# One result sum instead of two, and the expert loop's inputs fetched one unit earlier

## The chip, the cores and the metric

The kernel runs on one core of one Trainium2 chip. The time is the device time of a run in microseconds, the median of three runs. The profile is of one execution; its span goes from the first to the last instruction that was recorded.

## The reference

A batch of 16 sequences of 112 tokens of width 512 (1792 tokens) goes through two layers. The first is a cross-attention to 375 context rows, added to x. The second is a mixture of 64 experts:

```python
logits = x @ gate_weight.T                 # x is the layernormed token, 64 experts
top_val, top_idx = top_k(softmax(logits), 8)
rerouted = mapping[top_idx]                # the weaker 4 may be moved to a similar expert
gu = ragged_dot(xs, gate_up_proj)          # xs: the tokens of each expert, 512 -> 2*192
hact = silu(gate) * up
y = ragged_dot(hact, down_proj)            # 192 -> 512
out = zeros.at[tok].add(y * w)             # each token gets a sum over its experts
x = x + out
```

The last step is what the change is about: one token's row is added to by up to eight experts.

## The kernel before

**First part (0 to about 197 us).** The 16 sequences go through attention, gating and placing. SP stores x + attention to `out_rows` and the normed tokens to `normed_tokens`, and POOL enters each (token, weight) into the list of its expert in DRAM with 112 indirect DMAs (`enter`, L592).

**Second part, the expert loop.** Experts are ranked by how many tokens they have, and slot r of the program takes the expert of rank r. A *unit* is one expert: 17 units of three tiles (2 of 128 rows each, 8 of 112, 7 of 96) and then 46 of two tiles (17 of 128, 16 of 112, 12 of 96, 1 of 80). At the end a loop adds a tile of 128 rows for what did not fit (here one turn). All products are done in three passes on a high and a low part of each operand, so each unit needs its weights and tokens split: ACT copies the high part (`w1_high` L1052, `w2_high`, `x_high`, `h_high` L1030), DVE subtracts to get the low one (`w1_low` L909, `w2_low`, `x_low`, `h_low`).

For each unit:

- SP loads its list (`load_list`), its first weights `raw1` (768 KB, three DMAs, L484) and its second weights `raw2` (384 KB, L490 and L491).
- POOL gathers the tokens' rows into `xg` (L608). PE turns them (`turn_rows`), multiplies by the first weights in three groups m = 0, 1, 2 (`gate_up`, L1223 to L1225) and by the second (`down`).
- ACT takes `silu` of group 0 and of group 2, DVE multiplies (`h_gate` after group 1, `h_rest` L886 and L887 after group 2).
- ACT scales the result by the token's weight into `ys` (`y_out`, L1040), and POOL scatters `ys` with an indirect DMA that adds to DRAM (L617). `ys` has two buffers, so `y_out` of a unit waits until the scatter of the unit two before has landed.

The order on each engine is the order of the program: round r issues a stage of unit r, of r + 1 and so on, and an instruction that waits holds all behind it on its engine. Two adds to the same row may not be under way together. Before the change, units take turns between two sums: even ones add to `out_rows` (semaphore `scattered[0]`), odd ones to a second DRAM array `second_sum` (`scattered[1]`), which SP cleared in the first part. So the scatter of unit u waits for that of u - 2:

```python
def sums(self):
    return self.slot % 2
split_wait(pool, scattered[u.sums()], u.landed_before())
```

When all have landed, POOL adds `second_sum` to `out_rows` with one DMA of 3.5 MB (L644, `merged`), and the scatter of the last loop's tile (L638) waits for that. The code line above has a second effect: `load_list` of unit r + 4 reuses the list buffer of unit r - 4, waits until that unit's scatter has landed (L472), and stands on SP ahead of the weights of unit r + 2.

## Time and profile before

| | |
|---|---|
| median of three runs | 839.45 us (837.8 to 840.26) |
| profiled execution, first to last instruction | 805.3 us |
| PE, PEld, DVE, ACT, POOL busy | 676.6, 560.5, 541.6, 450.7, 516.2 us |
| mean granted TensorE clock | 0.936 |
| expert loop, first scatter to last scatter | 236.59 to 768.89 us |

The page gives the profiled execution's time as its span; the runs' own times hold some 34 us more (839.45 - 805.3), which lie before the first or after the last instruction. Busy shares are means over a first part that is bound by other things than the expert loop; the loop has to be read by stage.

### The profile page before, as it was taken

What the parts mean: (1) busy time and instruction counts of PE and PEld (TensorE: products, weight loads), DVE (VectorE), ACT (ScalarE), POOL (GpSimd) and SP (SyncE); (2) the same over time, 40 slices, a digit from 0 to 9 for tenths busy, and PEclk for the clock granted to TensorE, in tenths of its full rate; (3) what the DMA queues carried; (4) which work ended last, traced back from release to release, by engine and by line L of the source; (5) the groups of instructions that cost most, each with busy time, mean ns of one, the idle gap of its engine ahead of it and who ended that gap; (6) DMA issues with size and microseconds to landing.
All of it is one profiled execution on the core that took longest, in us unless ns stands there. A gap on an engine that the chain in (4) does not pass through costs nothing. (4 is left out here: it accounts for less than half of the span.)

```text
span 805.3 us, 15215 instructions
## 1 busy us (share of the span) xinstructions
PE 676.6 (84%) x4278; PEld 560.5 (70%) x4278; DVE 541.6 (67%) x1213; ACT 450.7 (56%) x891; POOL 516.2 (64%) x461
## 2 busy tenths in 40 slices
PE   4999999630599999999998998999988998989730
PEld 2555565320589999888988888878877977878630
DVE  5699898861276667776677777776767777767611
ACT  3444454310366666666775766757666676666610
POOL 6037777776738877887766666676657666666421
PEclk9999999855599999999999999999999999999965
DMA  8999999505659999999999999999999999999576
GB/s 304 349 313 332 322 330 301 170 12 159 177 154 220 244 240 237 239 247 255 247 268 256 268 241 259 245 245 258 236 260 217 250 236 245 233 246 232 107 132 152
DMA packets 107557, 189.93 MB, mean 236 GB/s; under 512 B 33521, under 2 KB 35441, under 8 KB 106065
## 3 DMA queue, kind: packets, MB, share of 16 engines
q1 hardware_dynamic: 74274, 125.61, 50.2%
q0 software_dynamic: 33200, 63.35, 38.9%
q8 instruction: 35, 0.57, 0.3%
q14 instruction: 48, 0.39, 0.2%
HBM read 143.40 MB, written 56.24 MB: 248 GB/s over the span
## 5 line engine op out<-in xcount | busy, mean ns | idle before, releaser
L1223 PE MATMUL bank<-xh,w1h 128*128 128x256 f32 (+7 forms) x768 | 229.3, 299 | 21.4 <-DVE h L887 21.2
L1224 PE MATMUL bank<-xl,w1h 128*128 128x256 f32 (+7 forms) x768 | 220.5, 287 | 0.0
L1225 PE MATMUL bank<-xh,w1l 128*128 128x256 f32 (+7 forms) x768 | 220.4, 287 | 0.0
L608 POOL DMA_INDIRECT xg<-normed_tokens,list x145 | 159.3, 1099 | 62.5 <-issue 55.9
L1223 PEld LDWEIGHTS bank<-xh,w1h 128*128 128x128 f32 x768 | 147.5, 192 | 27.0 <-issue 26.7
L617 POOL DMA_INDIRECT out_rows<-ys,list x73 | 116.7, 1599 | 72.9 <-ACT ys L1040 60.4
L903 DVE TENSOR_TENSOR xl<-bank,xh 128x448 fp32r<-128x448 f32 (+3 forms) x145 | 84.3, 616 | 115.1 <-ACT xh L1047 115.0
L592 POOL DMA_INDIRECT list_table<-token,slot x112 | 112.4, 1004 | 69.7 <-ACT token L1001 35.9
L617 POOL DMA_INDIRECT second_sum<-ys,list x70 | 111.2, 1589 | 64.5 <-ACT ys L1040 43.5
L1224 PEld LDWEIGHTS bank<-xl,w1h 128*128 128x128 f32 x768 | 147.9, 193 | 0.1
L1225 PEld LDWEIGHTS bank<-xh,w1l 128*128 128x128 f32 x768 | 147.6, 192 | 0.0
L909 DVE TENSOR_TENSOR w1l<-raw,w1h 128x1536 fp32r<-128x1536 f32 x65 | 114.5, 1762 | 39.9 <-ACT w1h L1052 39.9
L1205 PE MATMUL bank<-ident,xg 112*128 112x112 f32 (+3 forms) x580 | 76.7, 268 | 58.9 <-DMA xg<-normed_tokens,list 56.8
L1030 ACT CAST hh<-h 128x512 fp32r<-128x512 f32 (+6 forms) x64 | 39.0, 610 | 150.4 <-DVE h L887 150.4
L1205 PEld LDWEIGHTS bank<-ident,xg 112*128 112x128 f32 (+3 forms) x580 | 63.8, 144 | 76.3 <-DMA xg<-normed_tokens,list 42.0
L1052 ACT CAST w1h<-raw 128x1536 fp32r<-128x1536 f32 x65 | 97.4, 1499 | 6.4 <-DMA raw<-in_w 6.4
L1047 ACT CAST xh<-bank 128x448 fp32r<-128x448 f32 (+3 forms) x145 | 70.8, 537 | 47.6 <-PE bank L1205 47.6
L1040 ACT ACTIVATE ys<-bank,list 112x512 f32<-112x512 f32 (+3 forms) x143 | 89.3, 680 | 2.2 <-PE bank L1241 2.2
L894 DVE TENSOR_TENSOR hl<-h,hh 128x512 fp32r<-128x512 f32 (+6 forms) x64 | 43.5, 680 | 46.9 <-DVE h L887 44.9
L1236 PE MATMUL bank<-w2h,hh 128*112 128x512 f32 (+3 forms) x144 | 57.0, 396 | 5.5 <-DVE hl L894 5.5
L1241 PE MATMUL bank<-w2h,hl 128*112 128x512 f32 (+3 forms) x144 | 57.0, 396 | 0.0
L1238 PE MATMUL bank<-w2h,hl 128*112 128x512 f32 (+3 forms) x144 | 56.9, 395 | 0.0
(204 smaller groups left out, 1084.7 us busy)
## 6 DMA issues: line engine op xcount, KB each, us to landing
raw<-in_w SPq DMA_DIRECT2D x195, 256.0 KB, 4.7
raw<-in_w2a SPq DMA_DIRECT2D x65, 256.0 KB, 5.0
ctxT_s<-in_ctxT SPq DMA_DIRECT2D x16, 768.0 KB, 7.3
ctx_s<-in_ctx SPq DMA_DIRECT2D x16, 768.0 KB, 8.8
raw<-in_w2b SPq DMA_DIRECT2D x65, 128.0 KB, 5.9
list_table<-blank SPq DMA_DIRECT2D x30, 256.0 KB, 7.6
x_in<-in_x SPq DMA_DIRECT2D x16, 224.0 KB, 4.5
out_rows<-x SPq DMA_DIRECT2D x16, 224.0 KB, 8.8
```

What stands on the lines that cost most here:

```text
L592: pool.indirect_dma_start(table, bass.IndirectOffsetOnAxis(ap=slot8[b.four][:, k:k + 1], axis=0), token[b.four][:, k, :], None).then_inc(t ...
L608: pool.indirect_dma_start(xg[u.on(XGS)][0:u.m, t, :], None, normed, bass.IndirectOffsetOnAxis(ap=lists[u.on(LISTS)][0:u.m, t, 0:1], axis=0 ...
L617: pool.indirect_dma_start((out, second)[u.sums()], bass.IndirectOffsetOnAxis(ap=lists[u.on(LISTS)][0:u.m, t, 0:1], axis=0), ys[u.on(2)][0: ...
L903: v.tensor_tensor(xl[u.on(2)][:, :, part], turned(u, t), xh[u.on(2)][:, :, part].bitcast(F32), ALU.subtract).then_inc(xl_s, 1)
L909: v.tensor_tensor(w1l[u.on(2)][:].rearrange("p c f -> p (c f)"), raw1[u.on(RAW1)][:], w1h[u.on(2)][:].rearrange("p c f -> p (c f)").bitcas ...
L1040: a.activation(ys[u.on(2)][0:u.m, t, :], y_bank(u, t)[0:u.m, :], ACT.Copy, scale=of_row).then_inc(ys_s, 1)
L1047: a.copy(xh[u.on(2)][:, :, t * u.m:(t + 1) * u.m], turned(u, t)).then_inc(xh_s, 1)
L1052: a.copy(w1h[u.on(2)][:].rearrange("p c f -> p (c f)"), raw1[u.on(RAW1)][:]).then_inc(w1h_s, 1)
L1205: mm = pe.transpose(turned(u, t)[:, c, :], xg[u.on(XGS)][0:u.m, t, c * P:(c + 1) * P], ident[0:u.m, 0:u.m])
L1223: pe.matmul(bank[m][:, 0:W], wh, mh, start=(c == 0), stop=False)
L1224: pe.matmul(bank[m][:, 0:W], wh, ml, start=False, stop=False)
L1225: mm = pe.matmul(bank[m][:, 0:W], wl, mh, start=False, stop=(c == DK - 1))
```

## The change

- `second_sum`, its clearing, the merge and the second semaphore are gone. Every scatter adds to `out_rows`, and the scatter of a unit waits until **all** tiles of the units before it have landed. The last loop's scatter has a semaphore of its own (`over_added`).
- Buffers: `raw1` 3 to 4, `raw2` 2 to 3, lists 8 to 12, `xg` 3 to 4. SP loads lists 6 rounds ahead (4 before), `raw1` 4 (2), `raw2` 2 (1). POOL gathers 3 ahead (2).
- ACT and DVE split the first weights of unit r + 2 (r + 1 before), and do so late in the round. DVE does `h_rest` ahead of `w2_low`.
- PE's group m of a unit waits only for what frees its own bank; before, group 1 waited for all of `h` of the unit before.

The last three pieces below are DVE's order, ACT's order and PE's `gate_up`.

```diff
-SUM_TILES = [sum(nt for nt, m in RANKED[i::2]) for i in range(2)]
-RAW1, LISTS, XGS = 3, 8, 3
+RAW1, RAW2, LISTS, XGS = 4, 3, 12, 4
...
     def landed_before(self):
-        tiles = sum(nt for v, (nt, m) in enumerate(RANKED[:self.slot]) if v % 2 == self.slot % 2)
-        return tiles * 16 if not self.loop else (self.n - self.slot + tiles) * 16
+        return self.t0 * 16
...
-            for n in range(4):
+            for n in range(6):
                 load_list(Unit(n))
             for r in range(STATIC):
-                early_stage(load_list, r + 4)
-                if r > 0:
-                    early_stage(load_w1, r + 2)
-                early_stage(load_w2, r + 1) if r > 0 else None
+                early_stage(load_list, r + 6)
+                early_stage(load_w1, r + 4)
+                early_stage(load_w2, r + 2)
...
             def scatter(u):
-                split_wait(pool, scattered[u.sums()], u.landed_before())
+                wait(pool, scattered, u.landed_before())
                 for t in range(u.nt):
-                    pool.indirect_dma_start((out, second)[u.sums()], bass.IndirectOffsetOnAxis(ap=lists[u.on(LISTS)][0:u.m, t, 0:1], axis=0),
+                    pool.indirect_dma_start(out, bass.IndirectOffsetOnAxis(ap=lists[u.on(LISTS)][0:u.m, t, 0:1], axis=0),
...
             for r in range(STATIC + 2):
-                early_stage(gather, r + 2)
+                early_stage(gather, r + 3)
                 stage(scatter, r - 2)
...
-            for i in range(2):
-                pool.wait_ge(scattered[i], SUM_TILES[i] * 16)
-            pool.dma_start(out[0:TOK, :], second[0:TOK, :], accum_op=ALU.add, max_dma_last_dim=8192).then_inc(merged, 16)
...
             for r in range(STATIC):
                 early_stage(x_low, r + 1, (0, 1))
-                early_stage(w1_low, r + 1)
                 stage(h_gate, r)
                 early_stage(x_low, r + 1, (2,))
+                stage(h_rest, r)
                 stage(w2_low, r)
-                stage(h_rest, r)
+                early_stage(w1_low, r + 2)
                 stage(h_low, r)
...
             for r in range(STATIC):
                 early_stage(x_high, r + 1, (0, 1))
-                early_stage(w1_high, r + 1)
                 stage(silu_gate, r)
                 early_stage(x_high, r + 1, (2,))
                 stage(w2_high, r)
                 stage(silu_rest, r)
+                early_stage(w1_high, r + 2)
                 stage(h_high, r)
                 stage(y_out, r - 1)
...
-                if m == 0:
-                    wait(pe, silu_s, u.n * 2)
-                else:
-                    wait(pe, h_s, u.n * 3)
+                if u.loop or u.n > 0:
+                    if m == 0:
+                        pe.wait_ge(silu_s, u.n * 2 - 1)
+                    elif m == 1:
+                        pe.wait_ge(h_s, u.n * 3 - 2)
+                    else:
+                        pe.wait_ge(h_s, u.n * 3)
```

On POOL, in the middle of the expert loop (units of two tiles of 112 rows), three units in a row before; `ys`, `list` and `xg` carry their buffer's number, and the brackets hold the semaphores waited for:

```order
L617 DMA second_sum<-ys1,list5 1792x512 [waits ys_s,scattered1]
L617 DMA second_sum<-ys1,list5 1792x512 [waits ys_s]
L608 DMA xg0<-normed_tokens,list2 112x512 [waits xT_ps,list_in2]
L608 DMA xg0<-normed_tokens,list2 112x512
L617 DMA out_rows<-ys0,list6 1792x512 [waits ys_s,scattered0]
L617 DMA out_rows<-ys0,list6 1792x512 [waits ys_s]
L608 DMA xg1<-normed_tokens,list3 112x512 [waits xT_ps,list_in3]
L608 DMA xg1<-normed_tokens,list3 112x512
L617 DMA second_sum<-ys1,list7 1792x512 [waits ys_s,scattered1]
```

and the same place now:

```order
L598 DMA out_rows<-ys0,list0 1792x512 [waits ys_s,scattered]
L598 DMA out_rows<-ys0,list0 1792x512 [waits ys_s]
L589 DMA xg2<-normed_tokens,list6 112x512 [waits xT_ps,list_in6]
L589 DMA xg2<-normed_tokens,list6 112x512
L598 DMA out_rows<-ys1,list1 1792x512 [waits ys_s,scattered]
L598 DMA out_rows<-ys1,list1 1792x512 [waits ys_s]
L589 DMA xg3<-normed_tokens,list7 112x512 [waits xT_ps,list_in7]
L589 DMA xg3<-normed_tokens,list7 112x512
```

Scatters and gathers alternate as before, with the gather for one unit further ahead; what changed is that every scatter's first tile waits for the one `scattered`.

On ACT, at the same place before, one unit from `x_high` to `y_out`:

```order
L1047 CAST xh0<-bank4 128x4x96 [waits xT_ps,gu_ps]
L1047 CAST xh0<-bank3 128x4x96 [waits xT_ps]
L1052 CAST w1h0<-raw1_2 128x1536 [waits gu_ps,w1_in2]
L1019 ACTIVATE sg<-bank0 128x224 [waits h_s,gu_ps]
L1058 CAST w2h1<-raw2_1 128x512 [waits y_ps,w2_in1,gu_ps]
L1059 CAST w2h1<-raw2_1 64x512
L1024 ACTIVATE sg<-bank2 64x224 [waits gu_ps]
L1030 CAST hh1<-h 128x2x224 [waits y_ps,h_s]
L1040 ACTIVATE ys0<-bank7,list0 112x512 [waits y_ps,scattered0]
L1040 ACTIVATE ys0<-bank5,list0 112x512 [waits y_ps]
```

and now:

```order
L1031 CAST xh0<-bank4 128x4x96 [waits xT_ps,gu_ps]
L1031 CAST xh0<-bank3 128x4x96 [waits xT_ps]
L1001 ACTIVATE sg<-bank0 128x224 [waits h_s,gu_ps]
L1043 CAST w2h1<-raw2_1 128x512 [waits y_ps,w2_in1,gu_ps]
L1044 CAST w2h1<-raw2_1 64x512
L1006 ACTIVATE sg<-bank2 64x224 [waits gu_ps]
L1036 CAST w1h1<-raw1_3 128x1536 [waits gu_ps,w1_in3]
L1012 CAST hh1<-h 128x2x224 [waits y_ps,h_s]
L1024 ACTIVATE ys0<-bank7,list0 112x512 [waits y_ps,scattered]
L1024 ACTIVATE ys0<-bank5,list0 112x512 [waits y_ps]
```

The cast of the first weights (`w1h`) moved from ahead of the first `silu` to behind the second.

## Rows read from the trace of the kernel before

**Rows 1.** windows, by kind of unit (first scatter to first scatter)

```profile
core 0: us, PE busy (x) PEld busy (x) DVE busy (x) ACT busy (x) POOL busy (x), PEclk, DMA share, GB/s
236.59:401.83 165.24, 165.03 (x1076) 148.35 (x1075) 115.00 (x167) 114.55 (x202) 132.09 (x98) 1.00 1.01 239
401.83:545.62 143.79, 132.37 (x929) 119.18 (x928) 104.78 (x153) 96.27 (x172) 93.79 (x69) 1.00 1.01 255
545.62:676.74 131.12, 119.39 (x866) 106.10 (x866) 93.79 (x144) 87.24 (x162) 85.86 (x65) 0.99 0.98 242
676.74:767.18 90.44, 79.93 (x572) 68.64 (x571) 61.04 (x98) 58.48 (x111) 55.17 (x41) 0.98 0.87 206
```

**Rows 2.** timeline, one two-tile unit: start us, us, engine and line, what, idle before

```profile
501.67 0.62 ACT L1030 CAST hh<-h 128x512 fp32r<-128x512 f32 x1 [2.80 <-DVE h L887]
501.78 0.36 PE L1223 MATMUL bank<-xh,w1h 128*128 128x256 f32 x1 [0.80 <-DVE h L887]
502.20 1.26 ACT L1040 ACTIVATE ys<-bank,list 128x512 f32<-128x512 f32 x2
503.74 1.62 POOL L617 DMA_INDIRECT second_sum<-ys,list  x1 [2.09 <-ACT ys L1040]
504.29 1.51 ACT L1052 CAST w1h<-raw 128x1536 fp32r<-128x1536 f32 x1
505.83 1.76 DVE L909 TENSOR_TENSOR w1l<-raw,w1h 128x1536 fp32r<-128x1536 f32 x1 [0.51 <-ACT w1h L1052]
509.71 0.42 DVE L887 TENSOR_TENSOR h<-sg,bank 64x256 f32<-64x256 f32 x1
```

**Rows 3.** waits in the two-tile stages: who, for whom, us in total, times, longest

```profile
PE bank L1223 <- DVE h L887: 21.2, 30, 0.9
```

**Rows 4.** waits of the DMA queue on SP, same columns, 250 to 765 us

```profile
SPq L472 <- DMA second_sum<-ys,list: 46.2, 22, 3.0
SPq L472 <- DMA out_rows<-ys,list: 45.1, 24, 3.1
```

**Rows 5.** timeline, POOL and SP: a scatter's last tile, the next list load

```profile
497.19 1.59 POOL L617 DMA_INDIRECT out_rows<-ys,list  x1 [0.30 <-issue]
505.10 0.35 SPq L477 DMA_DIRECT2D list<-list_table  x1
...
646.25 1.49 POOL L617 DMA_INDIRECT out_rows<-ys,list  x1 [0.30 <-issue]
654.91 0.35 SPq L477 DMA_DIRECT2D list<-list_table  x1
...
637.99 1.49 POOL L617 DMA_INDIRECT second_sum<-ys,list  x1 [0.30 <-issue]
642.75 0.50 SPq L491 DMA_DIRECT2D raw<-in_w2b  x1
644.04 0.35 SPq L477 DMA_DIRECT2D list<-list_table  x1
```

**Rows 6.** timeline, POOL, the last scatter and the merge

```profile
768.89 1.41 POOL L617 DMA_INDIRECT out_rows<-ys,list  x1 [0.30 <-issue]
773.31 1.09 POOL L644 DMA_DIRECT2D out_rows<-second_sum  x1 [3.00 <-DMA out_rows<-ys,list]
```

**Rows 7.** chain that ended last, 766 to 806 us: start us, us, what

```profile
776.17 10.21 DMA list<-list_table
787.47 8.81 DMA xg<-normed_tokens,list
799.47 1.76 DVE w1l L909
```

**Rows 8.** one line's DMAs, list loads (first) and gathers: issue to landing

```profile
DMA to landing us min/median/max: 1.8/3.8/10.2
DMA to landing us min/median/max: 3.3/6.3/8.8
```

**Rows 9.** page, section 5: POOL's table entries in the first part

```profile
L592 POOL DMA_INDIRECT list_table<-token,slot x112 | 112.4, 1004 | 69.7 <-ACT token L1001 35.9
```

More of the change, by code:

```diff
@@ L121, in turn_of_tile @@
         return earlier if not self.loop else self.n - self.slot + earlier
-    def sums(self):
-        return self.slot % 2
     def landed(self, back):
-        upto = max(self.slot - back + 1, 0)
-        tiles = sum(nt for v, (nt, m) in enumerate(RANKED[:upto]) if v % 2 == (self.slot - back) % 2)
-        return tiles * 16
+        return TILES_BEFORE[max(self.slot - back + 1, 0)] * 16
     def landed_before(self):
-        tiles = sum(nt for v, (nt, m) in enumerate(RANKED[:self.slot]) if v % 2 == self.slot % 2)
-        return tiles * 16 if not self.loop else (self.n - self.slot + tiles) * 16
+        return self.t0 * 16
     def units_freed(self, ring):
@@ L196, in program @@
         row = sb("row", [P, 1])
-        zeros = sb("zeros", [P, D])
         blank = sb("blank", [P, BLANKS, LINE], I32)
@@ L223, in program @@
         raw1 = [sb(f"raw1_{i}", [P, DK * 2 * F]) for i in range(RAW1)]
-        raw2 = two("raw2_", [P, 2, D])
+        raw2 = [sb(f"raw2_{i}", [P, 2, D]) for i in range(RAW2)]
         w1h = [sb("w1h0", [P, DK, 2 * F], F32R)]
@@ L469, in load_list @@
                 else:
-                    wait(sp, scattered[u.sums()], u.landed(LISTS))
+                    wait(sp, scattered, u.landed(LISTS))
                 if u.slot < STATIC:
@@ L532, in _ @@
                                     pattern=[[-1, P]], channel_multiplier=1).then_inc(const_pool, 1)
-            nc.gpsimd.memset(zeros[:], 0.0).then_inc(const_pool, 1)
             nc.gpsimd.memset(blank[:], 0).then_inc(cleared, 1)
@@ L623, in _ @@
             gather(Unit(1))
+            gather(Unit(2))
             for r in range(STATIC + 2):
[L625 removed]
+                early_stage(gather, r + 3)
                 stage(scatter, r - 2)
             def keep_list(u):
[L629 removed]
+                split_wait(pool, list_in[u.on(LISTS)], (u.turn(LISTS) + 1) * 16)
                 nc.gpsimd.tensor_copy(over_list[:], lists[u.on(LISTS)][:, 0, 0:1]).then_inc(kept, 1)
@@ L1035, in y_out @@
                     split_wait(act, kept, (u.n - STATIC + 1) * KEPT)
-                wait(act, scattered[u.sums()], u.landed_before() if u.loop else u.landed(2))
+                    act.wait_ge(scattered, TILES_BEFORE[STATIC - 1] * 16)
+                else:
+                    wait(act, scattered, u.landed(2))
                 for t in range(u.nt):
```

66 lines of the change are left out of this document (32 added, 34 removed).

## The prediction, made before the result was known

> **What bounds the kernel now.** I read the waits and the windows by stage first, then the timeline of one unit, then SP's own waits, and the end of the chain last.
>
> While units have three tiles, PE is the bound: busy 165.03 of 165.24 us [rows 1]. In the three two-tile stages it is busy 132.37 of 143.79, 119.39 of 131.12 and 79.93 of 90.44 us, so 33.7 us are idle there, 21.2 of them before group 1 of `gate_up`, waiting for the `h` of the unit before [rows 3]. The timeline shows why [rows 2]. At 501.67 ACT starts `h_high`, then `y_out` and `x_high`, and the weight cast at 504.29 ends at 505.80; DVE's `w1_low` starts at 505.83, and the last `h` starts 3.9 us later at 509.71 and ends at 510.13, when the next `h_high` may start. That is a loop of ACT and DVE of 8.5 us, with nothing in it that PE or POOL could shorten. PE joins it with 0.80 us of idle.
>
> POOL waits too, 2.09 us for `ys`, but its scatters are not free [rows 2]. SP's list load waited 91.3 us in 46 places until a scatter had landed [rows 4]: landings come late. How late is read from the list load behind each wait. Without a wait, the list's DMA starts 0.79 us after the DMA ahead of it has been issued (642.75 + 0.50 = 643.25, then 644.04). So the scatter whose last tile was issued from 497.19 to 498.78 landed at 505.10 - 0.79 = 504.31, 5.5 us after its issue ended; the one of 647.74 landed at 654.12, 6.4 us after. Before 644.04 SP had not waited, so the tile issued until 639.48 (637.99 + 1.49) had landed by 643.25, at most 3.8 us after [rows 5]. The last scatter, with nothing else on the queues, landed no more than 3.0 us after 770.30 [rows 6]. The DMA engines' share is 1.01, 1.01, 0.98 and 0.87 [rows 1].
>
> **The change, part by part.** The sum is made on the span of 805.3 us and carried to the median of 839.45, since the 34 us outside the span hold none of the changed code.
>
> *One sum: the scatter chain.* Before, unit u waited for u - 2, which had two unit times to land. Now it waits for u - 1. From one scatter's start to the next there are then: (a) POOL's start after the wait ends. Not shown for this wait; the nearest is `ys`: first tile done at 502.20 + 0.68 = 502.88 (half of the 1.26 us and the overlap), scatter at 503.74, so 0.86 us [rows 2]. (b) The issue: 1.62 + 0.30 + 1.59 = 3.5 us for two tiles, 1.6 x 3 + 0.6 = 5.4 us for three [rows 2, 5]. (c) The landing L after the issue. The gathers, 2 or 3 of about 1.1 us, are issued inside L and cost nothing as long as L is over 3 to 4 us.
>
> L is the unknown. Its ends are 3.0 (empty queues) and 6.4 us. The samples under load lie at 5.5 and 6.4 with one at or under 3.8 [rows 5, 6]. I take 4.5, and 3.9 for the 96-row units, where the share is 0.87. That is below the middle of the loaded samples for two reasons. In a chain, no scatter packet is under way for some 3 us of each turn, which lets the weights through; and units come less often, which thins the load. Weights no longer stand behind the landing on SP (the list load waits for six units back), so they are issued when `w2_low` is done, about 7 us after the last `y_out`, and the 768 KB then run partly beside the next scatter. This is why I don't go lower.
>
> - 17 three-tile units: 0.86 + 5.4 + 4.5 = 10.76, times 17 = 182.9 us; before 165.2: +17.7.
> - 17 units of 2 x 128: 8.87, 150.8; before 143.8: +7.0.
> - 16 of 2 x 112 (issue 3.33): 8.69, 139.0; before 131.1: +7.9.
> - 12 of 2 x 96 (issue 3.2, L 3.9): 7.96, 95.5; before 90.4: +5.1.
>
> Together +37.7 us. Each 0.1 us of L is worth 62 x 0.1 = 6.2 us.
>
> The Trainium skill (DMA: Bandwidth & Descriptors, "Anatomy of one DMA — SWDGE (gpsimd) path") gives about 2.0 us plus bytes / 436e3 for a DMA from GpSimd, most of the 2 us being the receipt of the write; for a tile of 262 KB that is 2.6 us. The last scatter agrees with it (3.0 at most), the loaded ones don't (5.5, 6.4) [rows 5, 6]. With L = 2.6 the chain would be under PE's time everywhere, which is the first rival. The same page ("Latency and other measured facts") lets the access time of DRAM grow from 0.2 to 2 us at high load; that is in the sense of the loaded samples.
>
> *The reordering on ACT, DVE and PE.* It takes the weight cast and `w1_low` out of the loop of 8.5 us. What is left per unit of 2 x 128 is ACT's and DVE's own work: 96.27 / 17 = 5.7 and 104.78 / 17 = 6.2 us against PE's 132.37 / 17 = 7.8 [rows 1]. So PE would be the bound and 33.7 us would go. But the chain, 8.87 us, is longer than 7.8, so nothing of it is seen: `y_out` waits for the landing two units back, and ACT, then DVE, then PE stand behind it. With three tiles PE needs 165.03 / 17 = 9.7 us against the chain's 10.76. I cost this part at zero; it is worth up to -33.7 us if the chain is not the bound.
>
> *Fetching ahead.* Lists, weights and gathers are not what any long wait in the loop is for, so 0. At the start, PE does unit 0's group 0 before it turns unit 1's rows (up to -2 us), and 1.9 MB of weights instead of 0.8 run beside the first gathers (up to +2 us). I take 0. The SP stores of zeros and POOL's memset went from a part in which POOL's 112 table entries follow each other 1.3 us apart to the end (141 us; idle between them 33.8 without the first wait) [rows 9]: 0.
>
> *The end.* From 770.30, the end of the last scatter's issue, to 805.30 are 35.0 us: 3.0 of landing, the merge, then the over loop's bookkeeping for a next turn that is prefetched: list load 10.21, gather 8.81, then PE, ACT and DVE up to 801.23 [rows 6, 7]. Without the merge: POOL's copies and SP's list load come at once (776.17 - 773.31 = 2.9 after 770.30), the list takes 2.5 (between the least, 1.8, and the median, 3.8 [rows 8]), 1.1 to the gather (787.47 - 786.38), the gather 4 (least 3.3), 4.95 until `w1_low` ends, 4.07 to the end: 19.4, so -15.6 us. The last scatter lies beside this.
>
> Sum: 37.7 - 15.6 = +22: span 827, time 861 us.
>
> **Rivals.**
>
> 1. *The landing shortens to its unloaded value and PE becomes the bound.* The chain's turn for two tiles is under PE's 7.8 us if L is under 7.8 - 0.86 - 3.5 = 3.4. For it: the 3.0 us of the last scatter, the one of at most 3.8, and weights that are no longer bunched behind a landing. Against: a DMA share of 1.01 in all of the loop's first two stages [rows 1]; going from 8.5 to 7.8 us a unit asks for 9% more of it. Time: 839.45 - 33.7 - 15.6 - 1 = 789 us.
> 2. *The chain binds, but with L of 3.4 to 4.1.* The end's gain is larger than what the chain costs: 806 to 837 us.
> 3. *The chain binds with the landing as it is in the loaded samples, 5.1 or more*: 861 + 62 x 0.6 = 898 us. For it: two of three samples. Against: the load must fall when units come less often.
> 4. *No change:* the chain costs just what the end gives, L = 4.15 (0.35 less than 4.5).
>
> The forecast itself is the case on the slower side of the point where it turns: mean L above 4.15 us.
>
> **How the numbers follow.** Forecast, L from 4.2 to 5.0 (842 to 892 us): 0.50. Rival 1: 0.20. Rival 2: 0.14. Rival 3: 0.10. Rival 4: 0.06. The runs before spread over 2.5 us, so a change of 0.3% is about the least that can be told. Faster 0.34, same 0.06, slower 0.60. The range of 8 in 10 goes from 796, in the upper half of rival 1, to 893; the forecast's own range is 842 to 892.
>
> **What would show it.** If I am right, POOL's scatter waits mostly for a scatter's landing and no longer for `ys`; the turn from scatter to scatter is 10 to 11 us with three tiles and 8.4 to 9.2 with two, constant over widths where PE's would shrink; PE is idle already in the three-tile stages, and ACT's `ys` waits for a landing. The wait before group 1 for `h` is gone from the list in either case. If POOL waits for `ys` and PE stays 98% busy in the two-tile stages, rival 1 holds. The end from the last scatter is 19 us instead of 35 in all cases; over 25 would make that step wrong. The whole is wrong if the mean landing, read from scatter end to scatter start less 0.86, is under 4.1.

## The result, and the profile after

| | before | after |
|---|---|---|
| time, median (lowest to highest) | 838.62 us (837.38 to 840.26, 4 runs) | 868.30 us (865.72 to 871.27, 4 runs) |
| ratio after to before | | 1.0354, 95% interval 1.0326 to 1.0383 |

The change makes the kernel 3.5% slower: 868.3 us, where 861 was forecast.

The page of the kernel after: its span, then from section 4 the share of the span by engine and by line, then from section 5 the scatter, the first matmul of `gate_up`, the table entries and `y_out` (line, engine, tiles, count, busy us and mean ns, idle before and its releaser).

```profile
span 863.9 us, 15199 instructions
...
DMA 33%; PE 17%; issue 15%; DVE 15%; ACT 7%; another core or an unknown queue 7%; POOL 2%; SPq 2%; POOLq 0%; DVEq 0%; ACTq 0%
DMA out_rows<-ys,list 31%; ACT ys L1024 4%; DVE w1l L889 3%; PE bank L1214 2%; PE bank L1212 2%; POOL out_rows L598 2%; PE bank L1213 2%; PE bank L1191 2%; PE bank L1101 2%; DVE xl L883 1%; PE bank L1110 1%; ACT w1h L1036 1%; DVE of_entry L715 1%; DMA xg<-normed_tokens,list 1%
...
L598 POOL DMA_INDIRECT out_rows<-ys,list x143 | 220.8, 1544 | 176.6 <-ACT ys L1024 132.5
L1212 PE MATMUL bank<-xh,w1h 128*128 128x256 f32 (+7 forms) x768 | 227.7, 296 | 1.5 <-issue 1.5
...
L574 POOL DMA_INDIRECT list_table<-token,slot x112 | 108.8, 971 | 98.5 <-ACT token L983 68.6
...
L1024 ACT ACTIVATE ys<-bank,list 112x512 f32<-112x512 f32 (+3 forms) x143 | 89.8, 681 | 146.8 <-DMA out_rows<-ys,list 146.8
```

Nearly a third of the chain that ended last is the landing of scattered rows, `y_out` waited 146.8 us for landings and nothing else, and the wait of `gate_up` for `h` [rows 3] is gone: 1.5 us are left before L1212. PE now stands before `down` (L1225) instead: in the two-tile stages it waits 25.3 us there for DVE's `h_low`.

What that looks like in one place, in the two-tile stage of 112 rows, is in the timeline (start us, us, engine and line, what, idle before and releaser), by engine: POOL, then ACT, then SP's queue.

```profile
629.70 1.52 POOL L598 DMA_INDIRECT out_rows<-ys,list  x1 [2.05 <-ACT ys L1024]
631.53 1.50 POOL L598 DMA_INDIRECT out_rows<-ys,list  x1 [0.30 <-issue]
633.33 1.03 POOL L589 DMA_INDIRECT xg<-normed_tokens,list  x1 [0.30 <-issue]
634.67 1.08 POOL L589 DMA_INDIRECT xg<-normed_tokens,list  x1 [0.31 <-issue]
640.25 1.52 POOL L598 DMA_INDIRECT out_rows<-ys,list  x1 [4.50 <-ACT ys L1024]
642.08 1.50 POOL L598 DMA_INDIRECT out_rows<-ys,list  x1 [0.30 <-issue]
...
648.71 1.52 POOL L598 DMA_INDIRECT out_rows<-ys,list  x1 [2.46 <-ACT ys L1024]
...
639.33 1.26 ACT L1024 ACTIVATE ys<-bank,list 112x512 f32<-112x512 f32 x2 [4.96 <-DMA out_rows<-ys,list]
...
647.92 1.26 ACT L1024 ACTIVATE ys<-bank,list 112x512 f32<-112x512 f32 x2 [3.13 <-DMA out_rows<-ys,list]
...
631.73 1.39 SPq L468 DMA_DIRECT2D raw<-in_w  x3
...
638.51 1.37 SPq L468 DMA_DIRECT2D raw<-in_w  x3
```

The scatter issued until 631.53 + 1.50 = 633.03 has landed at 639.33, when ACT's waiting `ys` starts: 6.3 us. The next scatter starts 0.92 us later. Its own rows (issued until 643.58) land at 647.92, after 4.34 us, and the next scatter starts 0.79 us on. The row names `ys` as what POOL waited for. That is the profile's choice among two things that the same landing sets free: POOL's scatter and ACT's `ys` of the unit after.

What stands on SP differs between the two turns: two loads of the first weights are asked for in the first one (631.73 and 638.51), none between 640.25 and 648.71. The first weights (`raw1`) are called w1 from here on, the second ones w2.

The windows by kind of unit, from first scatter to first scatter, in the kernel after; before is in [rows 1].

```profile
core 0: us, PE busy (x) PEld busy (x) DVE busy (x) ACT busy (x) POOL busy (x), PEclk, DMA share, GB/s
278.00:459.10 181.10, 176.43 (x1147) 156.99 (x1146) 123.74 (x178) 121.72 (x211) 138.44 (x96) 1.00 0.95 229
459.10:613.35 154.25, 137.37 (x924) 116.71 (x923) 104.57 (x153) 95.59 (x171) 91.92 (x69) 1.00 0.95 236
613.35:752.58 139.23, 122.97 (x868) 103.43 (x866) 93.39 (x144) 86.62 (x161) 86.10 (x65) 1.00 0.92 229
752.58:842.25 89.67, 77.86 (x538) 64.69 (x538) 56.54 (x94) 54.22 (x106) 52.58 (x40) 0.96 0.73 162
```

Together 564.3 us for 62 units, 530.6 before, +33.7. But the two spans (805.3 and 863.9) differ by 58.6 us and the times by 29.7, so one of the profiles is unlike its timed runs. That was the first thing to settle.

### The profile page after: what moved, and what is told of

Read it like the earlier page. It is cut to its first block, busy times and chain, and to the rows that moved or that the text cites. A ratio compares the mean times of both kernels' runs of the same rounds, so it can differ in the third digit from the quotient of the medians.

```text
span 863.9 us, 15199 instructions
## 1 busy us (share of the span) xinstructions
PE 704.5 (82%) x4278; PEld 560.7 (65%) x4278; DVE 543.8 (63%) x1213; ACT 450.1 (52%) x891; POOL 516.6 (60%) x460
## 3 DMA queue, kind: packets, MB, share of 16 engines
q0 software_dynamic: 32736, 59.68, 33.7%
## 4 chain that ended last, share of the span: by engine, by line
DMA 33%; PE 17%; issue 15%; DVE 15%; ACT 7%; another core or an unknown queue 7%; POOL 2%; SPq 2%; POOLq 0%; DVEq 0%; ACTq 0%
DMA out_rows<-ys,list 31%; ACT ys L1024 4%; DVE w1l L889 3%; PE bank L1214 2%; PE bank L1212 2%; POOL out_rows L598 2%; PE bank L1213 2%; PE bank L1191 2%; PE bank L1101 2%; DVE xl L883 1%; PE bank L1110 1%; ACT w1h L1036 1%; DVE of_entry L715 1%; DMA xg<-normed_tokens,list 1%
## 5 line engine op out<-in xcount | busy, mean ns | idle before, releaser
L598 POOL DMA_INDIRECT out_rows<-ys,list x143 | 220.8, 1544 | 176.6 <-ACT ys L1024 132.5
L1212 PE MATMUL bank<-xh,w1h 128*128 128x256 f32 (+7 forms) x768 | 227.7, 296 | 1.5 <-issue 1.5
L589 POOL DMA_INDIRECT xg<-normed_tokens,list x145 | 170.8, 1178 | 59.4 <-issue 48.2
L574 POOL DMA_INDIRECT list_table<-token,slot x112 | 108.8, 971 | 98.5 <-ACT token L983 68.6
L1024 ACT ACTIVATE ys<-bank,list 112x512 f32<-112x512 f32 (+3 forms) x143 | 89.8, 681 | 146.8 <-DMA out_rows<-ys,list 146.8
L1212 PEld LDWEIGHTS bank<-xh,w1h 128*128 128x128 f32 x768 | 147.9, 193 | 2.0 <-issue 2.0
L1191 PE MATMUL bank<-ident,xg 112*128 112x112 f32 (+3 forms) x580 | 78.1, 268 | 56.6 <-DMA xg<-normed_tokens,list 34.1
L1191 PEld LDWEIGHTS bank<-ident,xg 112*128 112x128 f32 (+3 forms) x580 | 60.5, 143 | 84.9 <-issue 57.5
L1225 PE MATMUL bank<-w2h,hh 128*112 128x512 f32 (+3 forms) x144 | 62.5, 434 | 33.3 <-DVE hl L874 25.3
L1225 PEld LDWEIGHTS bank<-w2h,hh 128*112 128x112 f32 (+3 forms) x144 | 25.1, 174 | 51.8 <-DVE hl L874 27.6
L860 DVE TENSOR_TENSOR h<-sg,bank 128x256 f32<-128x256 f32 (+6 forms) x64 | 26.1, 408 | 51.1 <-issue 36.6
L1226 PE MATMUL bank<-w2l,hh 128*112 128x512 f32 (+3 forms) x144 | 57.2, 397 | 0.0
```

What stands on the lines that cost most here:

```text
L574: pool.indirect_dma_start(table, bass.IndirectOffsetOnAxis(ap=slot8[b.four][:, k:k + 1], axis=0), token[b.four][:, k, :], None).then_inc(t ...
L589: pool.indirect_dma_start(xg[u.on(XGS)][0:u.m, t, :], None, normed, bass.IndirectOffsetOnAxis(ap=lists[u.on(LISTS)][0:u.m, t, 0:1], axis=0 ...
L598: pool.indirect_dma_start(out, bass.IndirectOffsetOnAxis(ap=lists[u.on(LISTS)][0:u.m, t, 0:1], axis=0), ys[u.on(2)][0:u.m, t, :], None, co ...
L1024: a.activation(ys[u.on(2)][0:u.m, t, :], y_bank(u, t)[0:u.m, :], ACT.Copy, scale=of_row).then_inc(ys_s, 1)
L1191: mm = pe.transpose(turned(u, t)[:, c, :], xg[u.on(XGS)][0:u.m, t, c * P:(c + 1) * P], ident[0:u.m, 0:u.m])
L1212: pe.matmul(bank[m][:, 0:W], wh, mh, start=(c == 0), stop=False)
```

## The experiments

Each is timed beside the kernel before on the same chip; ratios are to that, with the 95% interval. All have three rounds if nothing else is said.

**Before, once more (`e1_before_again`).** No edit.

> The kernel before, unchanged, to set its timed runs beside a profile of the same kind. Theory A (what lies between the profiled span of 805.3 us and the time of 838.6 us is a first part, up to the first gather, that runs slower in the timed runs): the time lies 1.5 to 2.5 us above the span, as in the four runs of the changed kernel, the span is 834 to 838 us, and the table entries of a batch start 11.1 us after those of the batch before, not 8.8. Rival B (the 33 us lie outside the span): the span is 803 to 807 us, the batches 8.8 us apart, and the first part of the changed kernel is 26 us longer through its own edits.

Measured: 839.1 us, 0.9988 (0.9969 to 1.0006), span 835.7 in the profiled run; all its ten runs lie 1.7 to 1.9 us above their spans. Theory A holds; most batches of table entries start 11.1 us apart, where the first profile has 8.8 to 9.8. The row of page section 5 on the table entries, in this profile:

```profile
L592 POOL DMA_INDIRECT list_table<-token,slot x112 | 110.2, 984 | 99.3 <-ACT token L1001 69.4
```

99.3 us of idle before them against 69.7 [rows 9] and 98.5 in the kernel after. The profile that the prediction was read from had a first part some 30 us shorter than the timed runs. What made it so in that one execution no run here shows. This profile is the like one to compare with; its windows:

```profile
core 0: us, PE busy (x) PEld busy (x) DVE busy (x) ACT busy (x) POOL busy (x), PEclk, DMA share, GB/s
265.76:433.14 167.38, 165.20 (x1075) 148.34 (x1074) 115.52 (x167) 115.17 (x202) 133.02 (x97) 1.00 0.99 236
433.14:576.89 143.75, 131.50 (x929) 118.98 (x928) 104.78 (x153) 96.19 (x172) 93.74 (x68) 1.00 1.00 256
576.89:707.96 131.07, 118.42 (x866) 104.64 (x866) 93.80 (x144) 87.07 (x162) 85.82 (x64) 1.00 0.99 241
707.96:798.37 90.41, 79.67 (x584) 68.94 (x582) 61.06 (x98) 58.67 (x113) 55.14 (x41) 1.00 0.86 206
```

By it the 28.2 us between the spans are: start (to the first scatter) 265.8 to 278.0, +12.2; loop 532.6 to 564.3, +31.6; end (from the last scatter's issue) 34.1 to 18.6, -15.6.

**Two sums back (`e2_two_sums`).** In the kernel after:

```diff
-                    pool.indirect_dma_start(out, ...
+                    pool.indirect_dma_start((out, second)[u.sums()], ...
+            pool.dma_start(out[0:TOK, :], second[0:TOK, :], accum_op=ALU.add, ...).then_inc(merged, 16)
```

and the waits, zeros and clearing of before with it.

> The changed kernel with the two result sums and the merge put back, all else as changed (order of ACT, DVE and PE, fetching ahead, over unit's list taken without waiting for scatters). Theory A (the one chain of landings sets the pace of the changed kernel's expert loop): without it the loop falls to what PE and the short loop of ACT and DVE allow, from the first scatter to the last 495 to 515 us in place of 564, the wait of POOL for ys between scatters stays but that of ys for a landing goes, and the end grows from 18.5 to 25 to 30 us by the merge: 868 - 60 + 9 = about 817 us (805 to 830). Rival B (the new order on ACT, DVE and PE costs the time, the chain only follows): the loop stays at 555 to 570 us and the time is 868 + 9 = about 877 us (865 to 885).

Measured: 818.3 us, 0.9748 (0.9724 to 0.9772). Theory A holds for the loop; the windows of this kernel:

```profile
284.86:455.00 170.14, 165.72 (x1066) 146.79 (x1065) 116.50 (x168) 117.03 (x203) 133.61 (x97) 1.00 0.96 233
455.00:581.06 126.06, 126.06 (x920) 117.64 (x919) 104.88 (x154) 97.80 (x171) 103.87 (x68) 1.00 1.06 286
581.06:699.45 118.39, 118.31 (x900) 107.89 (x900) 96.20 (x149) 90.24 (x164) 96.75 (x64) 1.00 1.03 267
699.45:774.92 75.47, 74.57 (x561) 65.72 (x560) 58.07 (x94) 56.80 (x106) 58.32 (x39) 1.00 0.90 224
```

490.1 us in place of 564.3: the one chain of landings costs 74 us of loop, and with it gone PE is busy 126.06 of 126.06 us in the first two-tile stage. POOL hardly waits there either: its waits over 0.6 us come to 0.1 us a unit, the rest of the turn is its scatters, its gathers and the 0.3 us before each. Which of the two sets that turn no run separates. The landings themselves are longer than with one sum, 5.95 us with 2 x 128 and 6.60 with 2 x 112 on average, but `y_out` waits only 4.7 us in all for them in the two-tile stages. Wrong in both theories was the end: 38.2 us from the last scatter's issue, not 25 to 30. The merge takes 21.8 us from issue to landing (21.8 in e1's profile too), and the over unit's rows come behind it. Taking the over unit's list early does not shorten an end in which the merge stands: 38.2 us here, 34.1 before.

**One sum alone (`e3_before_one_sum`).** The kernel before, only with `out` as the one sum, `landed` and `landed_before` over all tiles, no merge, no clearing.

> The kernel before with one result sum and without the merge and the clearing, all else as before (order, depth of fetching ahead, scatter ahead of gather on POOL). Theory A (chain of landings): turns of 0.86 + issue + landing as in the changed kernel, 564 us (555 to 580) from first to last scatter in place of 531, the end some 9 to 14 us shorter than 35: 838.6 + 33 - 11 = about 861 us (850 to 875). Rival B (the order costs it): the loop stays near 531 us and the time falls by the merge alone, to about 828 us (822 to 835).

Measured: 904.9 us, 1.0772 (1.0708 to 1.0836): 615.4 us of loop, 17.6 of end. The direction is A's, the size neither's: this kernel is 37 us slower than the one with the whole change. So the other edits do give something back.

**A lighter w1 (`e4_light_w1`, one round).** In the kernel after:

```diff
+                    if u.n >= RAW1:
+                        part = slice(i * W1_PART, i * W1_PART + 128)
```

> The changed kernel, but from the fifth unit on each of the three transfers of w1 brings 128 columns of its third and not all, so that a unit moves 0.20 MB of w1 in place of 0.79 MB (the products are those of partly old weights; nothing else is left out). Theory A (a landing takes 4.0 to 5.2 us and not 2.7 because w1's transfer lies on it): landings 2.7 to 3.3 us after the issue ends, turns of 9.0 to 9.6 us with three tiles and 7.0 to 7.7 us with two, first to last scatter about 490 us (480 to 510) in place of 564 and the time about 795 us (785 to 815). Rival B (4 to 5 us is what the adding scatter itself takes in a running loop): landings 3.9 to 4.7 us as before, the time 868 us (860 to 872).

Measured: 829.5 us, 0.9883 (0.9851 to 0.9915), landings of 3.7 us in both large two-tile stages, loop 526.0 us. B falls, and A's size is half right: three quarters of w1's bytes are worth 0.8 to 1.0 us of a landing of 4.5 to 4.7. With 3 x 112 the landing falls by 0.5 us as well, but the turn only from 10.60 to 10.49. In the kernel after, the last six turns, for which no w1 is asked any more, show 2.5 to 2.8 us. What the rest of it belongs to (w2 and the gathers stayed) was not tried.

**Where the start went (`e5_start_order`).**

```diff
-                if r > 0:
-                    early_stage(turn_rows, r + 1, (0, 1))
+                early_stage(turn_rows, r + 1, (0, 1))
```

> The changed kernel with one part of its order on PE put back: the rows of unit 1's first two tiles are turned ahead of the first gate_up of unit 0, not all three behind it. The changed kernel's first scatter starts at 278.0 us, that of the kernel before (profiled anew) at 265.8. Theory A (this order costs the start: PE stands still before the turning of unit 2's last tile and unit 0's down comes late): the first scatter starts at 266 to 271 us, all behind it is as before, and the time is 857 to 862 us. Rival B (the start is late through the deeper fetching: two more lists, one more w1 and three more gathers ahead of the first unit's work): the first scatter stays at 276 to 280 us and the time at 866 to 870 us.

Measured: 868.7 us, 1.0324 (1.0283 to 1.0365), first scatter at 280.5: theory A falls. B's time is met, but this run does not show its reason. What the start does wait for shows in the timeline of the kernel after, DVE's and then PE's first row behind it.

```profile
260.83 0.56 DVE L866 TENSOR_TENSOR h<-sg,bank 64x384 f32<-64x384 f32 x1 [3.58 <-ACT sg L1006]
...
263.43 1.76 DVE L889 TENSOR_TENSOR w1l<-raw,w1h 128x1536 fp32r<-128x1536 f32 x1
265.10 0.95 DVE L874 TENSOR_TENSOR hl<-h,hh 128x768 fp32r<-128x768 f32 x1
266.08 1.16 DVE L883 TENSOR_TENSOR xl<-bank,xh 128x448 fp32r<-128x448 f32 x2
...
266.85 0.98 PE L1191 MATMUL bank<-ident,xg 112*128 112x112 f32 x4 [5.41 <-DVE xl L883]
```

PE stands 5.41 us until `x_low` of unit 2 frees the bank of its third tile, and `w1_low` now stands ahead of that `x_low`. The granted clock falls with it, to 0.63 on average from 258 to 272 us (1.2 GHz in two stretches of 3.4 and 6.8 us); in the kernel before, by e1's profile, it is 2.4 GHz from 246.5 us on.

**w1 asked for behind the scatter (`e6_late_w1`).** In the kernel after:

```diff
+                if not u.loop and u.n >= 8:
+                    sp.wait_ge(issued, u.n - 6)
...
+                nc.gpsimd.memset(mark[:, u.n:u.n + 1], 0.0).then_inc(issued, 1)
```

> The changed kernel, but w1 of unit u is asked for only after the last tile of scatter u - 7 is issued (a one-element memset on POOL behind each scatter tells SP), where the trace of the changed kernel has it 0.6 us after that scatter's start. All bytes are moved as before. Theory A (a landing takes 4.5 to 5 us because w1's packets stand ahead of the scatter's in the DMA engines): landings 3.0 to 3.7 us after the issue, turns of 7.6 to 8.2 us with two tiles and 9.6 to 10.1 with three, first to last scatter 520 to 535 us in place of 564 and a time of 825 to 840 us. Rival B (the engines' load as a whole sets the landing, wherever the w1 transfer stands): landings of 4 to 5 us, time 862 to 870 us. Rival C (w1 then comes late and PE waits for it): the wait of ACT or PE for w1 appears and the time is above 870 us.

Measured: 854.0 us, 1.0148 (1.0105 to 1.0191). Landings of 4.2 us in place of 4.7 and 4.5, loop 548.8 in place of 564.3. The same bytes, asked for 4.2 us after a scatter's start or later, cost less: A's mechanism, at a third to a half of its size. B's landings are met too, its time is not.

**A shorter start with two sums (`e7_two_sums_start`).** `e2_two_sums` with e5's edit, and on SP lists 0 to 2 ahead of w2 of unit 1 and of w1 of units 2 and 3.

> The changed kernel with two sums and the merge (818.3 us, first scatter at 284.9 us), and besides unit 1's first two tiles turned ahead of unit 0's first gate_up on PE, and on SP the first three lists loaded before w2 of unit 1 and w1 of units 2 and 3. Theory A (the start is lengthened by the PE order and by weight loads ahead of the lists on SP): the first scatter starts at 264 to 270 us and the time is 798 to 805 us. Rival B (the first units are bound by their gathers and weights): the first scatter stays beyond 278 us and the time at 812 to 820 us.

Measured: 813.5 us, 0.9677 (0.9635 to 0.9719), first scatter at 279.2. Both of B's ranges are met, by little (278 and 812 us). The first gather comes 5.8 us after the last table entry and not 12.0, and that is the gain of 5 us; from first gather to first scatter it still takes 42.8 us (44.3).

**Two sums at the old depth (`e8_two_sums_old_depth`).**

```diff
-RAW1, RAW2, LISTS, XGS = 4, 3, 12, 4
+RAW1, RAW2, LISTS, XGS = 3, 2, 8, 3
```

and each load and gather as far ahead as in the kernel before.

> The changed kernel with two sums and the merge, but with the buffers and the fetching of the kernel before: 3 w1, 2 w2, 8 lists, 3 gathers deep, in place of 4, 3, 12 and 4. It keeps the new order on ACT, DVE and PE, with the low and high parts of w1 made two units ahead. Theory A (the new order alone gives the gain of 41 us in the loop between the kernel before and the one with two sums, the fetching ahead gives nothing): first to last scatter 488 to 498 us, time 812 to 822 us. Rival B (the deeper fetching carries part of it): SP's, ACT's or POOL's waits for weights, lists or gathers return, 505 us or more from first to last scatter and a time of 828 us or more.

Measured: 830.2 us, 0.9866 (0.9826 to 0.9905), loop 517.5 us: theory B. With two sums the new order takes the loop from 532.6 to 517.5, the deeper fetching from there to 490.1. The profiled run of this kernel was its slowest (834.8 us, the others 828.5 to 830.5), so up to 5 us of its loop may be that run's own. And the depth that gives 27 us of loop gives 12 of time: the first scatter starts 9.3 us later with it (275.6 and 284.9).

**Two orders (`e9_two_orders`, five rounds).** `e7_two_sums_start`, with the old places of `w1_high`, `w1_low` and `w2_low` while r is below 17:

```diff
+                if r < THREES:
+                    early_stage(w1_low, r + 1)
                 stage(h_gate, r)
...
+                if r >= THREES - 1:
+                    early_stage(w1_low, r + 2)
```

> The kernel with two sums and the shorter start (813.5 us), with the order of ACT and DVE in the 17 three-tile units as in the kernel before (w1 one unit ahead and ahead of the gate, w2's low part ahead of h) and the changed order from there on. In the three-tile units the old order took 10.0 and 9.5 us a unit (profile of the kernel before), the new one 10.4 and 9.3, and the new one has PE stand before the turning of a third tile until DVE's xl, at the start for 5.5 us or more. Theory A (this wait costs the start and the 8 units of 3 x 112): first gather to first scatter 34 to 38 us in place of 42.8, the 3 x 112 units 10.0 us each, time 800 to 807 us. Rival B (the start is bound by lists, gathers and the clock, whatever the order): first gather to first scatter 41 to 45 us and 811 to 816 us.

Measured: 806.5 us (800.5 to 812.4, 6 runs), 0.9584 (0.9546 to 0.9621). First gather to first scatter 39.2 us (42.8 without it), the 17 three-tile units 167.9 us (170.1 in `e2_two_sums`): A in direction and time, though the start misses A's 34 to 38 us and the 3 x 112 units take 10.2 us. It is, with the next one, the fastest kernel here, 4.2% under the one before.

**The merge last (`e10_late_merge`, five rounds).** The merge's lines moved behind the loop over over units, whose rows then wait for the units' landings in `out_rows` and not for the merge.

> As e9_two_orders, but the merge is issued behind the loop over the over units, so that the last added rows of `out` go ahead of it and not behind. In the kernel with two sums the last landing is at 781 us, the merge is issued at 781.5 and has landed at 805.4, the over unit's rows are added behind it and the span ends at 816.3. Theory A (the merge takes its 24 us wherever it stands, and what stood behind it costs 8 to 11 us): the merge starts 5 to 7 us later and ends the span, 2 to 6 us less than e9_two_orders. Rival B (the over units' work is as long as what it saves): within 1.5 us of e9_two_orders. Rival C (beside fewer transfers the merge is shorter than 24 us): more than 6 us less.

Measured: 807.3 us, 0.9603 (0.9585 to 0.9620), no difference from `e9_two_orders`: rival B. The merge is issued at 778.5 and not 770.2, lands 20.2 us later (21.4 there), and the span ends 4.4 us after that. The 24 us that the expectation gives for the merge of `e2_two_sums` are not in its trace: it is issued at 781.45 and lands at 803.25.

**Gather ahead, one sum (`e11_gather_ahead`).** `e3_before_one_sum` with `XGS = 4` and:

```diff
-                early_stage(gather, r + 2)
+                early_stage(gather, r + 3)
                 stage(scatter, r - 2)
```

> The kernel before with one sum (904.9 us, 615 us from first to last scatter, PE waiting 170 us for gathered rows), and one edit of the change more: four buffers of gathered rows, and on POOL the gather of unit r + 3, not r + 2, ahead of the scatter of unit r - 2. Theory A (POOL stands in its queue before a scatter's landing wait with the next gather behind it, and one unit more of gathering ahead takes PE off that wait): PE's wait for gathered rows falls below 40 us, the chain of landings alone is left, 560 to 575 us from first to last scatter, and the time is 852 to 870 us. Rival B (the order of ACT and DVE is what holds the one-sum kernel back): 595 us or more and a time above 885 us.

Measured: 896.9 us, 1.0651 (1.0618 to 1.0683), loop 602.3. A falls: PE's wait for gathered rows is gone, but only 13 us of loop with it. B's number is met, but its reason is refuted by the next run. The clue is in SP's own waits from 300 to 830 us in this kernel (us in total, times, longest):

```profile
SPq L460 <- DMA out_rows<-ys,list: 194.9, 48, 6.7
```

and its timeline, SP's queue and then POOL:

```profile
607.35 0.35 SPq L465 DMA_DIRECT2D list<-list_table  x1
608.68 1.17 SPq L472 DMA_DIRECT2D raw<-in_w  x3
611.37 0.34 SPq L478 DMA_DIRECT2D raw<-in_w2a  x1
...
616.61 0.35 SPq L465 DMA_DIRECT2D list<-list_table  x1
...
607.41 1.60 POOL L601 DMA_INDIRECT out_rows<-ys,list  x1 [2.68 <-ACT ys L1021]
...
616.65 1.62 POOL L601 DMA_INDIRECT out_rows<-ys,list  x1 [2.25 <-ACT ys L1021]
```

One landing frees SP's list load and POOL's next scatter in the same instant (607.35 and 607.41). w1 stands behind the list on SP, so it is asked for 1.3 us after the scatter's start, unit after unit, and w2 behind it at 3.5 to 4.0.

**Lists ahead, one sum (`e12_lists_ahead`).** `e11_gather_ahead` with:

```diff
-RAW1, LISTS, XGS = 3, 8, 4
+RAW1, LISTS, XGS = 3, 12, 4
-                early_stage(load_list, r + 4)
+                early_stage(load_list, r + 6)
```

> As e11_gather_ahead (one sum, old order, 896.9 us, 602 us from first to last scatter), with one edit of the change more: 12 list buffers in place of 8 and each list fetched six units ahead, not four. In e11_gather_ahead SP waits 194.9 us for landings before its list loads, w1's load stands behind them and is asked for 1.3 us after nearly every scatter's start, and landings take 5.3 and 5.1 us (two tiles of 128 and 112 rows); in the changed kernel SP waits 7.8 us there, w1's phase drifts and they take 4.7 and 4.5. Theory A (the list wait locks w1's load onto the scatter and so lengthens the landing it waited for): SP's wait goes, w1's phase spreads, landings of 4.5 to 4.8 us, first to last scatter 565 to 582 us and a time of 855 to 876 us. Rival B (the remaining 38 us against the changed kernel are the order of ACT and DVE): landings as before or the turns no longer set by them, 592 us or more from first to last scatter and a time of 886 us or more.

Measured: 872.8 us, 1.0385 (1.0368 to 1.0403), loop 573.2: theory A. SP's waits in this kernel, over the same stretch:

```profile
SPq L451 <- DVE w2h L898: 93.2, 23, 6.3
SPq L460 <- DMA out_rows<-ys,list: 6.2, 22, 0.6
```

With SP no longer held by landings, it is w2's load that waits, for DVE to be done with its buffer. Landings fall from 5.3 and 5.1 us to 4.75 and 4.7 in the large two-tile stages, and over all units the shorter landings add up to the 29 us of loop. A had the wrong transfer, though. Outside the 3 x 112 units w1's phase hardly spreads (0.1 to 1.8 us in nearly all turns). It is w2 that moves, from 4.0 to 7.0 us after the scatter's start with 2 x 128 (medians), 3.7 to 6.8 with 2 x 112, where w1's median stays at 1.3, and 3.5 to 7.8 with 3 x 96, where the landing falls from 3.6 to 2.85. With 3 x 112 both loads spread over the turn (w1 0 to 8 us, w2 1.7 to 9.6, median 3.6 against 3.85), and the landing loses just 0.2. No run moves w2 alone, so that it is w2 is read from this agreement over the stages, not shown by a run of its own.

The landing in all one-sum kernels (mean from the end of the issue, by unit kind; the trace holds the time of each landing), and the two sides of the change as ladders:

| one sum | 3 x 112 | 2 x 128 | 2 x 112 | 2 x 96 | loop | time |
|---|---|---|---|---|---|---|
| before, one sum | 4.81 | 5.37 | 5.23 | 4.23 | 615.4 | 904.9 |
| + gather ahead | 4.36 | 5.28 | 5.09 | 4.40 | 602.3 | 896.9 |
| + lists ahead | 4.18 | 4.75 | 4.69 | 3.84 | 573.2 | 872.8 |
| + new order, w1 and w2 deeper (after) | 4.05 | 4.70 | 4.52 | 3.34 | 564.3 | 868.3 |
| after, w1 behind the scatter | 4.15 | 4.22 | 4.17 | 3.50 | 548.8 | 854.0 |
| after, a quarter of w1 | 3.56 | 3.67 | 3.69 | 3.12 | 526.0 | 829.5 |

With two sums: 839.1 before, 830.2 with the new order, 818.3 with the deeper fetching, 813.5 with the start, 806.5 with both orders. The kernels of a ladder were not all timed on the same chip; their ratios to the kernel before say the same, but the last step with one sum, from 1.0385 (1.0368 to 1.0403) to 1.0354 (1.0326 to 1.0383), is within its intervals.

## Why the prediction was right, point by point

**The bound of before.** Right: where the chain is not in the way, order and depth take the two-tile stages from 365 to 320 us (`e2_two_sums`), and PE is then busy all of it. But the loop of ACT and DVE was only half of what held them: the new order alone (`e8_two_sums_old_depth`) gives 18 us in the two-tile stages, not 33.7, and 15 in the loop. Nor were PE's 7.8 us for a unit of 2 x 128 a floor; `e2_two_sums` takes 7.42, so that rival 1, the case in which PE binds, would have given less than its 789 us. With three tiles PE was not the only bound. POOL does not wait once for more than 0.6 us in the 3 x 112 units of the kernel before: scatters 4.9, gathers 3.1 and the gaps between them 2.0 us make its whole turn of 10.0.

**The scatter chain.** The mechanism was right with two tiles. POOL's start behind a landing was taken as 0.86 us and is 0.8 to 0.9; the issue of two tiles, 3.5, is 3.52. The turns:

| | forecast L, turn | measured L, turn | forecast gain or loss | measured, to e1's profile |
|---|---|---|---|---|
| three tiles | 4.5, 10.76 | 4.05 (3 x 112), 10.65 | +17.7 | +13.7 |
| 2 x 128 | 4.5, 8.87 | 4.70, 9.07 | +7.0 | +10.5 |
| 2 x 112 | 4.5, 8.69 | 4.52, 8.70 | +7.9 | +8.2 |
| 2 x 96 | 3.9, 7.96 | 3.34, 7.47 | +5.1 | -0.7 |
| all | | | +37.7 | +31.6 |

The mean landing over the 62 turns is 4.24 us, so above the 4.1 to 4.15 at which it would have turned, by little. The largest miss is 2 x 96, where half of the landings, those with no w1 asked for beside them, take 2.5 to 2.8 us.

The value of L was near, the reasons for taking it under the samples were not. The two landings read as 504.31 and 654.12 are at 504.34 and 654.16 in the trace, so the reading was right; but they are of turns in which SP had to wait, and the means in that profile are 5.1 us (2 x 128) and 5.0 (2 x 112). The prediction lets L fall because a chain leaves the scatter's packets a pause and units come less often. `e3_before_one_sum` has that chain, with a turn of 9.85 us in place of 8.46, and its landings are 5.37 and 5.23 us, no shorter than before. They fall to 4.75 and 4.69 only with the lists ahead (`e12_lists_ahead`).

With 3 x 112 the turn of 10.60 is right for a wrong reason. POOL's start (0.82), issue and landing add up to 9.97 there, so a landing is not what comes last. It is POOL itself, in the kernel after (start us, us, idle before), between a last scatter tile and the next unit's first one:

```profile
336.81 1.48 POOL L598 DMA_INDIRECT out_rows<-ys,list  x1 [0.30 <-issue]
338.59 1.01 POOL L589 DMA_INDIRECT xg<-normed_tokens,list  x1 [0.30 <-issue]
339.91 1.14 POOL L589 DMA_INDIRECT xg<-normed_tokens,list  x1 [0.30 <-issue]
341.35 2.15 POOL L589 DMA_INDIRECT xg<-normed_tokens,list  x1 [0.30 <-issue]
343.99 1.53 POOL L598 DMA_INDIRECT out_rows<-ys,list  x1 [0.49 <-issue]
```

The rows had landed at 342.87, while POOL was still at the third gather. Over the eight units its longest idle time is 0.5 us, and scatters 4.5, gathers 4.2 and gaps 1.9 us make the whole turn. This is where the step failed by which the gathers "cost nothing as long as L is over 3 to 4 us": L is 4.05 and the gathers with their gaps take 5.5. It agrees with the two runs that shorten or move w1: with a landing of 3.56 us the turn is 10.49, and `e6_late_w1` has 10.66. PE, forecast to stand idle over the three-tile units, is busy 176.43 of 181.10 us, in part with the work of later units (1147 of its instructions are recorded there, 1075 in e1's profile).

**The reordering, costed at 0.** Right with one sum: from `e12_lists_ahead` to the kernel after, order and deeper w1 and w2 together are 4.5 us, within the intervals. The reason given, that the chain hides it, is what `e2_two_sums` shows by taking the chain away.

**Fetching ahead, costed at 0.** This step failed, though the sum hid it. The lists fetched further ahead are worth 24 us with one sum (896.9 to 872.8); they free SP from the landings, and w2 then goes out of the time in which a scatter's rows are under way. The gather one unit further ahead is worth another 8. The prediction had seen that weights no longer stand behind the landing on SP, but took it as a reason not to go lower with L, where the runs point to it as the reason for L being as low as it was. With two sums depth is worth 12 us of time. As a sum of edits it would have had to be +66 for one sum alone and -37 for the others; it came out because L was read for the kernel with both.

**The start, costed at 0 (between -2 and +2).** This step failed too: +12.2 us. The first gather comes 1.7 us later, and from it to the first scatter it takes 44.8 us and not 34.3. How the 10.6 us divide between order and depth stays open, since the two ladders do not agree. With two sums the new order at the old depth takes 41.2 us and depth brings it to 44.3. With one sum and the old order it takes 35.6, then 40.7 with the gather one unit further ahead and 42.5 with the lists, and the new order with deeper w1 and w2 adds only 2.3. So in the old order three more gathers ahead of the first scatter cost 5 us, a price that the prediction did not have; it counted weights alone, at up to 2. The one part of the order that was tried alone (PE's) is worth nothing, and the old order of ACT and DVE in the three-tile units gives back 3.6. What of it are waits for `xl` and what is the clock stays open.

**The end.** Forecast 19.4 us (its terms add up to 19.5) and -15.6, measured 18.6 us and -15.6 against e1's profile. The chain that ended last, in the kernel after (start us, us, what), has the terms that were summed:

```profile
845.36 0.20 POOL over_list L612
...
847.01 1.67 DMA list<-list_table
...
849.76 4.03 DMA xg<-normed_tokens,list
...
855.30 1.65 ACTq L143
856.98 1.76 DVE w1l L889
```

The list is asked for 1.65 us after the last issue (2.9 taken) and lands in 1.67 (2.5 taken), the gather takes 4.03 (4 taken), and from the end of `w1_low` to the end of the span it is 5.2 (4.07 taken). The path was right; that the difference is met to 0.1 us is chance, since the end before was 0.9 us shorter in e1's profile as well.

**The 34 us outside the span.** The prediction said that they hold none of the changed code. They were not outside: about 29 of them are a longer first part in the timed runs (first scatter at 236.6 and 265.8 us). It did little harm, since the terms came from the loop and the end.

**The sum.** It forecast +22 us of span; between profiles of the same kind it is +28.2. The loop came out 6 us under the forecast and the start 12 over it, and within the loop the three-tile units and 2 x 96 were taken too high, 2 x 128 too low. That 861 lies within 1% of 868.3 owes something to these misses going against each other.

**The rivals.** Rival 1's argument against itself was that the DMA engines have no room at a share of 1.01. `e2_two_sums` moves 286 GB/s in the stage where before moved 256. So a share of 1.01 was no bound on bytes. But the landings are 5.95 to 6.60 us at that rate, so the load counts too, besides the place of the transfers: `e6_late_w1` moves as many bytes as the kernel after and has shorter landings, `e4_light_w1` moves fewer and has the shortest. Rival 2's lower end of 806 us does not follow from its own rule of 6.2 us for 0.1 us of L, which gives 793 for L = 3.4.

## What to carry to other kernels

When a chain of read-modify-write transfers is made to wait for each landing, price its turn as start + issue + landing and take the landing under load; check that the engine that issues the chain is free when the landing comes, its other transfers counted in; then ask what else the same landing sets free, because a transfer that it releases may lie on the next landing, every turn. A second accumulator, which gives each scatter two turns to land, was worth 74 us of loop here; its merge and the longer start took 24 of them back (818.3 against 868.3 us). And compare the span of a profile with the times first: if the difference is not that of the other runs (1.7 to 1.9 us here), the profile is of another execution than the timed ones, and the first task is to find in which part.

## What the runs showed of the hardware

- The adding scatter of two tiles of 112 rows lands 3.7 us after its issue beside a quarter of w1 (means), 4.5 beside all of it, 5.2 with w1 and w2 asked for 1.2 and 3.7 us after its start, and 6.6 with two sums at 267 GB/s. One of two tiles of 96 rows takes 2.5 to 2.8 with no w1 asked for any more. The Trainium skill (DMA: Bandwidth & Descriptors, "Anatomy of one DMA — SWDGE (gpsimd) path") gives the rule by which the prediction's estimate for a tile of 128 rows was 2.6 us, and by which an estimate for one of 96 rows is 2.45. The last turns agree with it; every mean under load is above it.
- The DMA engines' busy share was 1.00 at 256 GB/s (e1's profile) and 1.06 at 286 (`e2_two_sums`), over the same 17 units of 2 x 128.
- POOL has 0.30 us of idle before each indirect DMA that it issues back to back, and a scatter tile takes it 1.5 to 1.6 us, a gather 1.0 to 1.1 (some 2.15): eight units of three tiles of 112 rows keep it at work for the whole turn of 10.6 us.
- Asking for 0.79 MB of w1 some 3 to 4 us later in the turn, with not a byte less, is worth 14 us (`e6_late_w1`, units 8 on).
- A merge of 3.67 MB of DRAM into DRAM with addition took 20.2 to 22.3 us from issue to landing in seven profiles, 21.8 in three of them.
